# Key products of two edge groups: two 64-column products beside each other instead of two summed 128-column products with zeros

## The chip, the cores and the metric

The program runs on one core of one Trainium2 chip. Its engines work from queues of their own: TensorE (PE, with weight loads shown apart as PEld), VectorE (DVE), ScalarE (ACT), GpSimd (POOL), and SyncE (SP), which here only issues DMAs. They wait for one another through semaphores. The metric is the device time of one execution in microseconds. The kernel before takes 5307.28 us, the median of 3 runs (5303.45 to 5312.74).

## The reference, cut to what matters

A graph network with 6250 nodes and 206,250 edges (100,000 drawn edges, their mirror images and one loop for each node, sorted by destination). The first layer runs five rounds of message passing and a layer norm; the change doesn't touch it. The second layer is attention over edges:

```
def _conv_per_edge(x_src, edge_attr, edge_sh, Wang, Wlin, W1, b1, W2):
    rad = relu(edge_attr @ W1 + b1) @ W2          # b1: 64 wide, W2k: 64 x 64, W2v: 64 x 128
    g = edge_sh @ Wang.T
    return x_src * g @ Wlin * rad                 # Wlin_k: 128 x 64, Wlin_v: 128 x 128
k = _conv_per_edge(x[src], edge_attr, edge_sh, Wang_k, Wlin_k, W1k, b1k, W2k)   # keys, 64 per edge
v = _conv_per_edge(x[src], edge_attr, edge_sh, Wang_v, Wlin_v, W1v, b1v, W2v)   # values, 128 per edge
alpha = einsum('ehq,qk,ehk->eh', q[dst], Wdot, k)     # 8 heads
# softmax of alpha over the edges of one dst, then the weighted sum of v
```

So each edge has a key of 64 numbers, itself the elementwise product of two matrix products: the "radial" one, relu(...) @ W2k, and the "linear" one, (x * g) @ Wlin_k.

## The kernel before, in words

`edge_attention` works on 404 groups of 512 edges (GE = 512), with an edge in each column. Two groups make a pair, and there are 202 pairs. Since a key has 64 numbers and a tile has 128 partitions, the keys of a pair share a tile: those of the first group lie on partitions 0 to 63, those of the second on 64 to 127. From there on one instruction handles the keys of 1024 edges: the copy to `rad_k` (L2265), the products with `rad_k` and with the query (L2373, L2376), and the product that sums each head and puts it into a row of `b_s` (L2158).

To fill such a shared tile, TensorE does two products over all 128 columns of its array and sums them in the bank `b_k`. The weights stand in the middle of a tile of 192 columns with zeros on both sides. The slice for the first group has the 64 weight columns first and 64 zero columns after them, the slice for the second the other way round. `radial_k` (L2126) does this with `w2k` and `hidden` (rows 64 to 127 of `w2k` are zeros, because `hidden` holds the 64 hidden units of the keys and below them those of the values), `linear_k` (L2134) with `wlin_k` and `x_gk`. Both write `b_k`: the radial product of pair p is copied to `rad_k` by ACT, then the linear product of pair p takes the bank, and DVE reads it at L2373 (semaphore `p_lk` tells it that the product is done, `p_rk` tells the same of the radial product to ACT).

The order on every engine is written out by hand, pair by pair (`for i in range(LAST)`). For one pair TensorE does: turn the gathered rows (L2096), gates (L2105, L2108), hidden layer (L2114), linear keys of the pair before (L2134), turn an output (L2166), turn rows again, linear values (L2142), radial values (L2119), gates, turn queries (L2148), hidden layer, linear and radial values, head sums (L2158), turn an output, and radial keys (L2126). A 32-bit product of 512 columns shows as two MATMUL records, each with a LDWEIGHTS of its own; a call for both groups at L2126 or L2134 is thus four records.

Every 8 pairs a round of softmax work runs for 16 groups, mostly on DVE: scans (L2418, L2449, L2468, L2493), a reciprocal (L2499) and others. Four times in a round TensorE does a tiny product in between, at L2175 (`collect`) or L2183 (`hand_out`). Values wait 16 pairs for their weights and are then weighed and summed (L2394, L2402), so at the end there are 16 pairs' worth of such work without key products.

The built program marks each product with a piece of the array, as rows x columns. In the kernel before that is the whole array, 128 x 128, for every product of this stage but two: 128 x 32 at L2175 and 32 x 128 at L2183.

Of the kernel before, what the change touches and what calls it, by code (L numbers as in the profile page):

```python
# [18 lines left out]
P = 128  # L19
D = 128  # L20
DQ = 64
H = 8
EA = 16
HID = 64
# [1776 lines left out]
def edge_attention(nc, a, parts, x1_table, q_first, same_row, sums_table, ident, lent, G):  # L1801
# [31 lines left out]
    with ExitStack() as ctx:  # L1833
        def sb(name, shape, dt=F32):
            return ctx.enter_context(nc.sbuf_tensor(f"e_{name}", shape, dt))
# [11 lines left out]
        gates_part = [sb(f"gates_part{n}", [6 * EA, 3 * D], BF16) for n in range(3)]  # L1847
        gates_less = [sb(f"gates_less{n}", [6 * EA, 3 * D]) for n in range(2)]
        stack = sb("stack", [6 * EA, 3 * D], BF16)
        wlin_k = sb("wlin_k", [D, 3 * DQ])  # L1850
        wlin_v = sb("wlin_v", [D, D])
        b1 = sb("b1", [2 * HID, 1])
        w2k = sb("w2k", [2 * HID, 3 * DQ])
        w2v = sb("w2v", [2 * HID, D])
        ones = sb("ones", [P, P])
        gather_heads = sb("gather_heads", [P, 2 * P])
# [15 lines left out]
        hidden = several("hidden", 2, [2 * HID, GE])  # L1872
        x_gk = several("x_gk", 4, [D, GE])
# [33 lines left out]
        b_k = bank("b_k")  # L1907
# [65 lines left out]
        def _(sp):  # L1973
# [4 lines left out]
            for n, name in enumerate(("wang_k_t", "wang_v_t", "W1")):  # L1978
                for r in range(6):
                    sp.dma_start(gates[r * EA:(r + 1) * EA, n * D:(n + 1) * D], a[name]).then_inc(w_in, 16)  # L1980
            sp.wait_ge(const, 3)
            sp.dma_start(wlin_k[:, DQ:2 * DQ], a["Wlin_k"]).then_inc(w_in, 16)
            sp.dma_start(w2k[0:HID, DQ:2 * DQ], a["W2k"]).then_inc(w_in, 16)
            sp.dma_start(w2v[HID:2 * HID, :], a["W2v"]).then_inc(w_in, 16)
            sp.wait_ge(cut, 5)
            for n, r0, r1 in ((0, 0, 3), (1, 3, 4), (2, 4, 5), (1, 5, 6)):
# [62 lines left out]

        @block.gpsimd  # L2050
        def _(pool):
            nc.gpsimd.memset(wlin_k[:], 0.0).then_inc(const, 1)
            nc.gpsimd.memset(w2k[:], 0.0).then_inc(const, 1)
            nc.gpsimd.memset(w2v[:], 0.0).then_inc(const, 1)
            nc.gpsimd.memset(ones[:], 1.0).then_inc(const, 1)
            nc.gpsimd.memset(gather_heads[:], 0.0).then_inc(const, 1)
            nc.gpsimd.memset(minus_big[:], -BIG).then_inc(const, 1)
            nc.gpsimd.memset(across[0][:, 0:1], -BIG).then_inc(const, 1)
            nc.gpsimd.memset(wacross[0][:, 0:1], 0.0).then_inc(const, 1)
            pool.wait_ge(const, 8)  # L2060
            own_rows = gather_heads[:, P - ROWS:P]
            nc.gpsimd.affine_select(out=own_rows, in_=ones[:, 0:ROWS], compare_op=ALU.is_ge, fill=0.0, base=0,
                                    pattern=[[-H, ROWS]], channel_multiplier=1).then_inc(const, 1)
            pool.wait_ge(const, 9)
            nc.gpsimd.affine_select(out=own_rows, in_=own_rows, compare_op=ALU.is_ge, fill=0.0, base=H - 1,
                                    pattern=[[H, ROWS]], channel_multiplier=-1).then_inc(const, 1)
            nc.gpsimd.affine_select(out=row_of_head[:].rearrange("k (g h) -> k g h", h=H),
                                    in_=ones[0:H, :].rearrange("k (g h) -> k g h", h=H), compare_op=ALU.is_equal,
                                    fill=0.0, base=0, pattern=[[0, ROWS], [1, H]], channel_multiplier=-1
                                    ).then_inc(const, 1)  # L2070
            pool.wait_ge(w_in, n_w)
            for g in range(G):
                if g >= 3:
                    pool.wait_ge(p_x, g - 2)
                for j in range(GT):
                    nc.gpsimd.indirect_dma_start(  # L2076
                        x_rows[g % 3][:, j, :], None, x1_table,
                        bass.IndirectOffsetOnAxis(ap=src[:, g * GT + j:g * GT + j + 1], axis=0)
                        ).then_inc(x_got[g % 3], 16)

        @block.tensor
        def _(pe):
            pe.wait_ge(const, 11)
            nc.tensor.transpose(b_x[:, 0:H], row_of_head[:], ident[0:H, 0:H]).then_inc(p_small, 1)
            pe.wait_ge(w_in, n_w)
            pe.wait_ge(stacked, 64)
            pe.wait_ge(const, 12)

            def turn_x(g):
                pe.wait_ge(x_got[g % 3], 64 * (g // 3 + 1))  # L2090
# [30 lines left out]
            def radial_k(p):  # L2121
                pe.wait_ge(a_hid, 2 * p + 2)
                if p > 0:
                    pe.wait_ge(v_key, p)
                for half in range(2):
                    mm = nc.tensor.matmul(b_k[:], w2k[:, (1 - half) * DQ:(1 - half) * DQ + P], hidden[half][:],  # L2126
                                          start=(half == 0), stop=(half == 1))
                mm.then_inc(p_rk, 1)

            def linear_k(p):  # L2130
                pe.wait_ge(v_g, 4 * p + 3)
                pe.wait_ge(a_rk, p + 1)
                for half in range(2):
                    mm = nc.tensor.matmul(b_k[:], wlin_k[:, (1 - half) * DQ:(1 - half) * DQ + P],  # L2134
                                          x_gk[(2 * p + half) % 4][:], start=(half == 0), stop=(half == 1))
                mm.then_inc(p_lk, 1)

            def linear_v(g):
                pe.wait_ge(v_g, 2 * g + 2)
# [98 lines left out]
        @block.scalar  # L2238
        def _(act):
            act.wait_ge(w_in, n_w)  # L2240
            act.wait_ge(const, 8)

            def copy_x(g):
                act.wait_ge(p_x, g + 1)
# [4 lines left out]
            def hide(g):  # L2249
                act.wait_ge(p_hid, g + 1)  # L2250
                if g >= 2:
                    act.wait_ge(p_rk, g // 2)
                nc.scalar.activation(hidden[g % 2][:], b_r[:], ACT.Relu, bias=b1[:, 0:1]).then_inc(a_hid, 1)  # L2253

            def copy_rv(g):
# [3 lines left out]
                nc.scalar.copy(rad_v[g % 3][:], b_r[:]).then_inc(a_rv, 1)  # L2259

            def copy_rk(p):
                act.wait_ge(p_rk, p + 1)
                if p >= 2:
                    act.wait_ge(v_key, p - 1)
                nc.scalar.copy(rad_k[p % 2][:], b_k[:]).then_inc(a_rk, 1)  # L2265
# [64 lines left out]

        @block.vector
        def _(dve):
            dve.wait_ge(const, 8)
            dve.wait_ge(w_in, n_w)
            rest = gates
            for n in range(3):
# [13 lines left out]
            def gated(g):  # L2350
                dve.wait_ge(p_g, 2 * g + 1)
                dve.wait_ge(a_x, g + 1)
                if g >= 4:
                    dve.wait_ge(p_lk, g // 2 - 1)
                nc.vector.tensor_tensor(x_gk[g % 4][:], b_gk[:], x_t[g % 2][:], ALU.mult).then_inc(v_g, 1)  # L2355
                dve.wait_ge(p_g, 2 * g + 2)
                if g >= 4:
                    dve.wait_ge(p_lv, g - 3)
                nc.vector.tensor_tensor(x_gv[g % 4][:], b_gv[:], x_t[g % 2][:], ALU.mult).then_inc(v_g, 1)
# [6 lines left out]
                nc.vector.tensor_tensor(value[g % KEPT], b_lv[:], rad_v[g % 3][:], ALU.mult).then_inc(v_value, 1)  # L2366

            def products(p):
                dve.wait_ge(p_lk, p + 1)
                dve.wait_ge(a_rk, p + 1)  # L2370
                if p >= 2:
                    dve.wait_ge(p_score, p - 1)
                nc.vector.tensor_tensor(prod[p % 2][:], b_k[:], rad_k[p % 2][:], ALU.mult).then_inc(v_key, 1)  # L2373
                dve.wait_ge(v_key, p + 1)
                dve.wait_ge(v_query, 2 * p + 2)
                nc.vector.tensor_tensor(prod[p % 2][:], prod[p % 2][:], q_t[p % 2][:], ALU.mult).then_inc(v_prod, 1)  # L2376
# [259 lines left out]
```

## Time and profile before

| | |
|---|---|
| runs | 5303.45, 5307.28, 5312.74 us |
| the profiled execution's own time | 5309.66 us |
| its span in the trace | 5307.9 us |
| PE busy, share of the span | 4432.0 us, 83% |
| PE weight loads | 2894.7 us, 55% |
| DVE busy | 3888.6 us, 73% |
| ACT busy | 2422.2 us, 46% |
| POOL busy | 2022.3 us, 38% |
| edge attention, pair work | about 2510 to 5135 us of the span |

The shares are means over stages that have different limits. The change is inside the edge attention, so what matters is read there. A record of TensorE is longer than the time for which it holds the array: products are pipelined, so a product's cost in a full queue is the distance from its start to the next one's start, not its length. "Idle before" and the name behind the arrow tell how long an engine stood still and what ended that; small gaps of TensorE are hidden by the records' length.

### The profile page before, as it was taken

To read this page: it belongs to the slowest core of one execution; us is meant where nothing else is said; L and a number is where in the kernel's file an instruction comes from. 1 tells how busy PE (TensorE), PEld (TensorE's weight loads), DVE (VectorE), ACT (ScalarE), POOL (GpSimd) and SP (SyncE) were. 2 spreads that over 40 slices of the span, in tenths; PEclk is the share of its full clock that TensorE was granted. 3 is DMA by queue.
4 is the path that set the end of the run, shared out by engine and by line. 5 is a ranking of instruction groups with operands and counts; after the bars stand their busy time and mean duration, and the time that the engine had idled before them with its cause. 6 is when DMAs were issued, how large, how long until landed. Compare 5 with 4: busy or idle time off the path is not lost. (4 is left out here: it accounts for less than half of the span.)

```text
span 5307.9 us, 66619 instructions
## 1 busy us (share of the span) xinstructions
PE 4432.0 (83%) x19382; PEld 2894.7 (55%) x19382; DVE 3888.6 (73%) x6001; ACT 2422.2 (46%) x3740; POOL 2022.3 (38%) x1942
## 2 busy tenths in 40 slices
PE   4666689899999999741999999999999999999823
PEld 4666577777777777630445445544544454544412
DVE  7999654545545454441689999999998999999945
ACT  5666555554545545330444444444444444444411
POOL 3333000000000000015766666666666666766422
PEclk9888899999999999855999999999999999999955
DMA  3333699998999989403599999999999999999961
GB/s 109 103 103 101 143 221 219 197 229 184 222 193 222 227 182 232 83 0 79 140 230 249 256 246 257 249 247 254 254 246 241 251 248 244 256 247 241 241 179 35
DMA packets 1847237, 1043.13 MB, mean 197 GB/s; under 512 B 1316550, under 2 KB 1666372, under 8 KB 1846892
## 3 DMA queue, kind: packets, MB, share of 16 engines
q1 hardware_dynamic: 1441835, 700.05, 59.8%
q10 hardware_dynamic: 344208, 211.90, 13.7%
q0 software_dynamic: 60848, 127.02, 9.1%
q8 instruction: 163, 2.67, 0.2%
q14 instruction: 183, 1.49, 0.1%
HBM read 763.53 MB, written 274.94 MB: 196 GB/s over the span
## 5 line engine op out<-in xcount | busy, mean ns | idle before, releaser
L2076 POOL DMA_INDIRECT e_x_rows<-x_table,e_src x1616 | 1682.5, 1041 | 824.5 <-issue 438.9
L1144 PE MATMUL acc<-t_wide,scaled 128*128 128x512 f32 (+1 forms) x6370 | 1466.2, 388 | 120.5 <-DVE t_wide L1281 75.6
L1144 PEld LDWEIGHTS acc<-t_wide,scaled 128*128 128x128 f32 x6370 | 1165.7, 191 | 406.9 <-ACT t_wide L1162 137.6
L1162 ACT CAST t_wide<-t_ring 128x1176 fp32r<-128x1176 uint8 (+1 forms) x490 | 597.0, 1255 | 303.1 <-PE acc L1144 212.9
L1281 DVE CAST t_wide<-t_ring 128x1764 fp32r<-128x1764 uint8 (+1 forms) x490 | 535.0, 1124 | 223.5 <-PE acc L1144 220.2
L1647 POOL MEMSET l_eps<- 128x1 f32 x2 | 0.2, 102 | 1648.3 <-POOLq L1347 1639.6
L2402 DVE TENSOR_TENSOR_SCAN e_vsum<-e_factors,e_vsum,e_weighted 128x512 f32<-128x512 f32 x403 | 519.2, 1288 | 14.2
L539 PE MATMUL lists_rows_ps<-lists_hot_lo,lists_hot_hi 128*128 128x196 fp8e4 x3200 | 377.4, 286 | 177.3 <-DVE lists_hot_hi L464 177.3
L2271 ACT COPY e_out_rows<-e_b_o 128x512 f32<-128x512 f32 x404 | 236.8, 586 | 564.4 <-PE e_b_o L2166 436.9
L2142 PE MATMUL e_b_lv<-e_x_gv,e_wlin_v 128*128 128x512 f32 x808 | 431.1, 615 | 72.6 <-DVE x_res L2366 38.2
L1291 DVE TENSOR_TENSOR e_less<-e_x,e_part 128x512 f32<-128x512 f32 x101 | 69.9, 692 | 548.9 <-ACT e_part L1184 336.6
L539 PEld LDWEIGHTS lists_rows_ps<-lists_hot_lo,lists_hot_hi 128*128 128x128 fp8e4 x3200 | 338.4, 110 | 215.7 <-DVE lists_hot_hi L464 198.7
L2119 PE MATMUL e_b_r<-e_hidden,e_w2v 128*128 128x512 f32 x808 | 445.6, 634 | 0.8 <-ACT e_hidden L2253 0.8
L2259 ACT COPY e_rad_v<-e_b_r 128x512 f32<-128x512 f32 x404 | 237.0, 587 | 425.2 <-PE e_b_r L2119 425.0
L2355 DVE TENSOR_TENSOR e_x_gk<-e_b_gk,e_x_t 128x512 f32<-128x512 f32 x404 | 275.3, 681 | 170.0 <-PE e_b_gv L2108 115.6
L2134 PE MATMUL e_b_k<-e_x_gk,e_wlin_k 128*128 128x512 f32 x808 | 385.4, 599 | 13.2 <-ACT e_rad_k L2265 13.0
L330 ACT CAST lists_staged<-lists_rows_ps 128x784 uint8<-128x784 f32 x400 | 312.5, 812 | 183.8 <-PE lists_rows_ps L539 183.0
L2126 PE MATMUL e_b_k<-e_hidden,e_w2k 128*128 128x512 f32 x808 | 380.3, 593 | 0.0
L2166 PEld LDWEIGHTS e_b_o<-ident,e_vsum 128*128 128x128 f32 x1616 | 208.0, 148 | 313.7 <-issue 176.9
L2253 ACT ACTIVATE e_hidden<-e_b_r,e_b 128x512 f32<-128x512 f32 x404 | 278.9, 690 | 146.7 <-PE e_b_r L2114 144.4
L2247 ACT COPY e_x_t<-e_b_x 128x512 f32<-128x512 f32 x404 | 237.8, 589 | 223.2 <-PE e_b_x L2096 131.4
L2166 PE MATMUL e_b_o<-ident,e_vsum 128*128 128x128 f32 x1616 | 262.9, 288 | 88.0 <-DVE e_vsum L2402 37.9
(207 smaller groups left out, 6250.4 us busy)
## 6 DMA issues: line engine op xcount, KB each, us to landing
e_factors<-share_rows SPq DMA_DIRECT2D x404, 512.0 KB
sums_table<-e_out_rows ACTq DMA_DIRECT2D x404, 256.0 KB
t_ring<-adjacency_bytes SPq DMA_DIRECT2D x245, 416.5 KB, 6.2
t_ring<-adjacency_bytes SPq DMA_DIRECT2D x245, 367.5 KB, 4.8
q_first<-hop_zeros_q ACTq DMA_DIRECT2D x101, 512.0 KB, 4.5
e_q_rows<-q_first SPq DMA_DIRECT2D x404, 128.0 KB
e_same_dst<-same_row SPq DMA_DIRECT2D x404, 128.0 KB
adjacency_bytes<-lists_staged SPq DMA_DIRECT2D x196, 196.0 KB, 2.7
```

What stands on the lines that cost most here:

```text
L330: nc.scalar.copy(staged[g % 3][:, at * half:(at + 1) * half, :], rows_ps[t % 3][:, :, 0:2 * LO]).then_inc(evicted, 1)
L539: mm = nc.tensor.matmul(rows_ps[t % 3][:, side, col * LO:(col + 1) * LO], his[:, i * P - i % 2 * SLOTS:i * P - i % 2 * SLOTS + P], los[:, ...
L1144: mm = nc.tensor.matmul(acc[c][:, 0:n], U[p][:, b, :], flat_t[:, lo:lo + n], start=(b == 0 and p == 0), stop=(b == NB - 1 and p == 1), ski ...
L1162: nc.scalar.copy(wide[g % WIDE][:, h0:h1, :], ring[g % BYTES][:, h0:h1, :]).then_inc(wide_act, 1)
L1281: nc.vector.tensor_copy(wide[g % WIDE][:, 0:h1, :], ring[g % BYTES][:, 0:h1, :]).then_inc(wide_dve, 1)
L2076: nc.gpsimd.indirect_dma_start(x_rows[g % 3][:, j, :], None, x1_table, bass.IndirectOffsetOnAxis(ap=src[:, g * GT + j:g * GT + j + 1], axis=0)
L2119: nc.tensor.matmul(b_r[:], w2v[:], hidden[g % 2][:], start=True, stop=True).then_inc(p_rv, 1)
L2126: mm = nc.tensor.matmul(b_k[:], w2k[:, (1 - half) * DQ:(1 - half) * DQ + P], hidden[half][:], start=(half == 0), stop=(half == 1))
L2134: mm = nc.tensor.matmul(b_k[:], wlin_k[:, (1 - half) * DQ:(1 - half) * DQ + P], x_gk[(2 * p + half) % 4][:], start=(half == 0), stop=(half ...
L2142: nc.tensor.matmul(b_lv[:], wlin_v[:], x_gv[g % 4][:], start=True, stop=True).then_inc(p_lv, 1)
L2166: tr = nc.tensor.transpose(b_o[:, j * P:(j + 1) * P], vsum[g % 3][:, j * P:(j + 1) * P], ident[:])
L2402: nc.vector.tensor_tensor_scan(out=vsum[g % 3][:], data0=factors[g % FACTORS][:, 1, :], data1=weighted[g % 2][:], initial=vsum[(g - 1) % 3 ...
```

## The change

The tiles `wlin_k` and `w2k` lose their zeros: `wlin_k` is now 128 x 64, `w2k` 64 x 64. Each half of the pair is a product of its own with 64 output partitions: the first group's goes to partitions 0 to 63 of `b_k`, the second group's to 64 to 127. Nothing is summed in the bank any more, and each half raises the semaphore, so that the waits on `p_rk` and `p_lk` count twice as far. The built program marks the radial halves with pieces of 64 x 64 at row 0, columns 0 and 64, and the linear halves with pieces of 128 x 64 at columns 0 and 64. The number of columns that stream (512 for each half) is as before, and so is the number of products.

No instruction changes place on PE, DVE, ACT or SP; on POOL two memsets fall away at the start of the stage, with the counts on `const`.

```diff
-        wlin_k = sb("wlin_k", [D, 3 * DQ])
+        wlin_k = sb("wlin_k", [D, DQ])
-        w2k = sb("w2k", [2 * HID, 3 * DQ])
+        w2k = sb("w2k", [HID, DQ])
...
-            sp.wait_ge(const, 3)
-            sp.dma_start(wlin_k[:, DQ:2 * DQ], a["Wlin_k"]).then_inc(w_in, 16)
-            sp.dma_start(w2k[0:HID, DQ:2 * DQ], a["W2k"]).then_inc(w_in, 16)
+            sp.wait_ge(const, 1)
+            sp.dma_start(wlin_k[:], a["Wlin_k"]).then_inc(w_in, 16)
+            sp.dma_start(w2k[:], a["W2k"]).then_inc(w_in, 16)
...
-            nc.gpsimd.memset(wlin_k[:], 0.0).then_inc(const, 1)
-            nc.gpsimd.memset(w2k[:], 0.0).then_inc(const, 1)
             nc.gpsimd.memset(w2v[:], 0.0).then_inc(const, 1)
...
                 for half in range(2):
-                    mm = nc.tensor.matmul(b_k[:], w2k[:, (1 - half) * DQ:(1 - half) * DQ + P], hidden[half][:],
-                                          start=(half == 0), stop=(half == 1))
-                mm.then_inc(p_rk, 1)
+                    nc.tensor.matmul(b_k[half * DQ:(half + 1) * DQ, :], w2k[:], hidden[half][0:HID, :], start=True,
+                                     stop=True).then_inc(p_rk, 1)
...
                 for half in range(2):
-                    mm = nc.tensor.matmul(b_k[:], wlin_k[:, (1 - half) * DQ:(1 - half) * DQ + P],
-                                          x_gk[(2 * p + half) % 4][:], start=(half == 0), stop=(half == 1))
-                mm.then_inc(p_lk, 1)
+                    nc.tensor.matmul(b_k[half * DQ:(half + 1) * DQ, :], wlin_k[:], x_gk[(2 * p + half) % 4][:],
+                                     start=True, stop=True).then_inc(p_lk, 1)
...
-                    act.wait_ge(p_rk, g // 2)
+                    act.wait_ge(p_rk, 2 * (g // 2))
...
-                act.wait_ge(p_rk, p + 1)
+                act.wait_ge(p_rk, 2 * p + 2)
...
-                    dve.wait_ge(p_lk, g // 2 - 1)
+                    dve.wait_ge(p_lk, 2 * (g // 2 - 1))
...
-                dve.wait_ge(p_lk, p + 1)
+                dve.wait_ge(p_lk, 2 * p + 2)
```

## Rows read from the trace of the kernel before

**Rows 1.** Busy time by stretch of the span, columns in the first line.
```profile
core 0: us, PE busy (x) PEld busy (x) DVE busy (x) ACT busy (x) POOL busy (x), PEclk, DMA share, GB/s
2620.00:5020.00 2400.00, 2287.09 (x8595) 1183.94 (x8594) 2212.13 (x3220) 1073.65 (x1837) 1594.59 (x1526) 0.98 1.00 246
```
**Rows 2.** TensorE in order of time: start, us, line, out<-in, shape, count.
```profile
4001.58 1.13 PE L2119 MATMUL e_b_r<-e_hidden,e_w2v 128*128 128x512 f32 x2
4002.54 1.02 PE L2158 MATMUL e_b_s<-e_prod,e_gather_heads 128*128 128x512 f32 x2
4003.40 0.60 PE L2166 MATMUL e_b_o<-ident,e_vsum 128*128 128x128 f32 x4
4003.84 1.88 PE L2126 MATMUL e_b_k<-e_hidden,e_w2k 128*128 128x512 f32 x4
4005.56 0.60 PE L2096 MATMUL e_b_x<-ident,e_x_rows 128*128 128x128 f32 x4
...
4006.64 1.88 PE L2134 MATMUL e_b_k<-e_x_gk,e_wlin_k 128*128 128x512 f32 x4
4008.36 0.60 PE L2166 MATMUL e_b_o<-ident,e_vsum 128*128 128x128 f32 x4
```
**Rows 3.** Timeline of the weight loads beside the first of these.
```profile
4003.73 0.30 PEld L2126 LDWEIGHTS e_b_k<-e_hidden,e_w2k 128*128 128x128 f32 x2
4004.27 0.19 PEld L2126 LDWEIGHTS e_b_k<-e_hidden,e_w2k 128*128 128x128 f32 x1 [0.24 <-issue]
```
**Rows 4.** Timeline of TensorE around the gates, without a tiny product.
```profile
3999.77 0.38 PE L2108 MATMUL e_b_gv<-e_sh_t,e_stack 96*128 96x512 bf16 x1
3999.98 0.60 PE L2148 MATMUL e_b_x<-ident,e_q_rows 128*128 128x128 f32 x4
```
**Rows 5.** Timeline of TensorE one pair later, with one (L2175).
```profile
4010.10 1.02 PE L2119 MATMUL e_b_r<-e_hidden,e_w2v 128*128 128x512 f32 x2
4010.95 0.38 PE L2105 MATMUL e_b_gk<-e_sh_t,e_stack 96*128 96x512 bf16 x1
4011.18 0.38 PE L2108 MATMUL e_b_gv<-e_sh_t,e_stack 96*128 96x512 bf16 x1
4011.48 0.21 PE L2175 MATMUL e_b_o<-e_ends,e_head_of_row 128*8 128x16 f32 x2
4011.62 0.66 PE L2148 MATMUL e_b_x<-ident,e_q_rows 128*128 128x128 f32 x4
```
**Rows 6.** Timeline of VectorE over one round: all its waits of 0.1 us or more.
```profile
4090.37 0.69 DVE L2355 TENSOR_TENSOR e_x_gk<-e_b_gk,e_x_t 128x512 f32<-128x512 f32 x1 [2.19 <-PE e_b_gv L2108]
...
4101.65 0.69 DVE L2355 TENSOR_TENSOR e_x_gk<-e_b_gk,e_x_t 128x512 f32<-128x512 f32 x1 [1.12 <-PE e_b_gv L2108]
...
4124.58 0.69 DVE L2355 TENSOR_TENSOR e_x_gk<-e_b_gk,e_x_t 128x512 f32<-128x512 f32 x1 [0.64 <-PE e_b_gv L2108]
...
4127.96 0.69 DVE L2366 TENSOR_TENSOR feats<-e_b_lv,e_rad_v 128x512 f32<-128x512 f32 x1 [0.17 <-PE e_b_lv L2142]
...
4161.36 0.69 DVE L2355 TENSOR_TENSOR e_x_gk<-e_b_gk,e_x_t 128x512 f32<-128x512 f32 x1 [0.90 <-PE e_b_gv L2108]
...
4164.74 0.69 DVE L2366 TENSOR_TENSOR feats<-e_b_lv,e_rad_v 128x512 f32<-128x512 f32 x1 [0.17 <-PE e_b_lv L2142]
```
**Rows 7.** The same for TensorE, the gaps that its records leave open.
```profile
4142.37 1.10 PE L2142 MATMUL e_b_lv<-e_x_gv,e_wlin_v 128*128 128x512 f32 x2 [0.63 <-DVE feats L2366]
...
4157.79 0.66 PE L2166 MATMUL e_b_o<-ident,e_vsum 128*128 128x128 f32 x4 [0.91 <-DVE e_wacross L2478]
...
4181.33 1.92 PE L2142 MATMUL e_b_lv<-e_x_gv,e_wlin_v 128*128 128x512 f32 x2 [2.61 <-DVE x_res L2366]
```
**Rows 8.** Busy time of three stretches of that round, columns as in Rows 1.
```profile
4084.00:4128.00 44.00, 43.91 (x168) 23.18 (x167) 39.25 (x59) 20.82 (x36) 28.86 (x27) 0.98 1.10 265
...
4164.70:4181.30 16.60, 14.00 (x56) 7.05 (x54) 16.35 (x22) 7.06 (x12) 12.58 (x13) 1.00 0.82 228
4181.30:4187.70 6.40, 6.37 (x14) 2.94 (x15) 6.22 (x9) 1.17 (x2) 1.18 (x2) 0.73 0.83 196
```
**Rows 9.** Waits in the stretch 2620 to 5020: in total, times, longest.
```profile
SPq L1993 <- PE e_b_r L2114: 946.5, 165, 12.6
...
POOL e_x_rows L2076 <- PE e_b_x L2096: 372.3, 175, 7.2
...
ACT e_out_rows L2271 <- DMA sums_table<-e_out_rows: 84.2, 39, 5.0
```
**Rows 10.** Timeline of the start of the stage.
```profile
2490.56 0.26 POOL L2052 MEMSET e_wlin_k<- 128x192 f32 x1 [11.27 <-POOLq L1522]
2490.76 0.26 POOL L2053 MEMSET e_w2k<- 128x192 f32 x1
...
2500.82 0.42 SPq L1982 DMA_DIRECT2D e_wlin_k<-in_Wlin_k  x1
```

More of the change, by code:

```diff
@@ L2059, in _ @@
             nc.gpsimd.memset(wacross[0][:, 0:1], 0.0).then_inc(const, 1)
-            pool.wait_ge(const, 8)
+            pool.wait_ge(const, 6)
             own_rows = gather_heads[:, P - ROWS:P]
@@ L2063, in _ @@
                                     pattern=[[-H, ROWS]], channel_multiplier=1).then_inc(const, 1)
-            pool.wait_ge(const, 9)
+            pool.wait_ge(const, 7)
             nc.gpsimd.affine_select(out=own_rows, in_=own_rows, compare_op=ALU.is_ge, fill=0.0, base=H - 1,
@@ L2082, in _ @@
         def _(pe):
-            pe.wait_ge(const, 11)
+            pe.wait_ge(const, 9)
             nc.tensor.transpose(b_x[:, 0:H], row_of_head[:], ident[0:H, 0:H]).then_inc(p_small, 1)
@@ L2086, in _ @@
             pe.wait_ge(stacked, 64)
-            pe.wait_ge(const, 12)
+            pe.wait_ge(const, 10)
             def turn_x(g):
@@ L2240, in _ @@
             act.wait_ge(w_in, n_w)
-            act.wait_ge(const, 8)
+            act.wait_ge(const, 6)
             def copy_x(g):
@@ L2332, in _ @@
         def _(dve):
-            dve.wait_ge(const, 8)
+            dve.wait_ge(const, 6)
             dve.wait_ge(w_in, n_w)
```

## The prediction

> **What bounds the kernel now.** The change lives in the pair work of the edge attention, so I first read the busy time by stretch [rows 1]. From 2620 to 5020 us TensorE is busy 2287 of 2400 us, VectorE 2212, and the DMA share is 1.00. All three are nearly full, so neither engine's share alone says what a shorter product is worth. Next come the waits of the two engines over one round of 8 pairs, 4084 to 4187 us [rows 6, 7]. An engine that waits shows that the other one is the limit just before. VectorE waits for TensorE at 4090, 4101, 4124 and 4161 (2.19, 1.12, 0.64, 0.90 us). TensorE waits for VectorE at 4142, 4157 and 4181 (0.63, 0.91, 2.61 us). The limit therefore changes hands inside a round: TensorE sets the pace from 4084 to 4128, where it is busy 43.91 of 44.00 us [rows 8], and from 4157.8 to 4164.7; VectorE sets it in the other stretches, with its scans and its reciprocal. The waits of the other queues come last [rows 9]: SP waits 946 us for TensorE before it loads more features, POOL 372 us, so transfers mostly follow TensorE. Only the output stores hold somebody up (84 us in 39 waits).
>
> **What a pair of key products costs now.** In a full queue the distance between starts counts, not the length. L2126 starts at 4003.84, the next line at 4005.56: 1.72 us for four records, 0.43 each; L2134 has the same, 4006.64 to 4008.36 [rows 2]. The next record's weight load lies under the running one (loads at 4003.73 and 4004.27, [rows 3]) and costs nothing. There are two such sets in a pair, so 3.44 us of some 12 us.
>
> **What the change does to the streams.** It leaves the number of records and their 512 columns. A half that uses 64 of 128 columns of the array streams as long as before. Time is saved only if the array runs records of the two halves at the same time. A half is two records on the same piece of the array, which must follow each other (0.43 + 0.43). Records start in the order of the queue: first half, first half, second half, second half. So the third can start beside the second at best, the fourth after the third: three steps of 0.43 = 1.29 instead of 1.72. Saved: 0.43 a set. If the third record's 64-column weight load can't be taken in earlier, it comes on top. A 128-column load that isn't hidden costs 1.13 - 1.02 = 0.11 us (L2119 after a wait against L2119 in a full queue, [rows 2, 5]); half the columns make it 0.05. The trace has no two pieces at work at once; the bounds are 1.29 (all overlaps as said) and 1.72 (nothing does).
>
> **What the change adds: switching the piece.** The trace has this already, at the tiny products. Without one, L2148 follows L2108 after 0.21 us [rows 4]. With L2175 in between it follows after 0.44 us, and the four L2148 take 0.66 instead of 0.60, a load that isn't hidden: together the detour costs 0.29 us [rows 4, 5]. Of this the streaming is two records of 16 columns, 2 x 0.43 x 16/512 = 0.03. The rest, 0.26, is two changes of piece, with an 8-column load open on the way in. A 64-column load is some 0.04 dearer by the 0.11 above. So 0.30 us for going in and out, at each set. The neighbours of a set are always whole-array products: L2166 or L2158 before L2126, L2096 after it, L2114 before L2134, L2166 or L2096 after it. Between the halves nothing else stands, and I take no change there. The bounds of this term are 0.26 and, if each entry and exit cost the whole detour, 0.58; the nearest row gives 0.30, and that I take. Before, none of it was paid.
>
> The page TensorEngine Tiling (Array Packing) of the Trainium skill, section Tiling Modes, says that changing the mode, not just the piece, drains the engine. By that rule the same four drains a pair come out, and the trace agrees with its 0.29. The same page's table of theoretical speedup promises up to 2x for a side of 64; that would halve the 1.72 and is a rival below.
>
> **The sum.** A set goes from 1.72 to 1.29 + 0.30 = 1.59, or 1.64 with the third load open: saved 0.08 to 0.13, say 0.10 us. In the round above, the sets (L2126 and L2134, eight each) that lie where TensorE sets the pace are eight between 4084 and 4128 and two between 4157.8 and 4164.7: 10 of 16. The other six end in a TensorE wait for VectorE, which only gets longer. There are 202/8 = 25.25 rounds: 10 x 0.10 x 25.25 = 25 us, bounds 20 and 33. VectorE can follow: what is taken is its own waits, 5.2 us a round. If all 16 sets counted, at 0.13, it would be 53 us.
>
> Other edits: two memsets of 0.26 us leave POOL at 2490.56, where SP comes to L1982 only at 2500.82, long after [rows 10]: nothing. The doubled semaphore counts move no wait, since every waiting instruction still waits for the second half. The order of the queues is as before. The copy of `rad_k` and the DVE products start 0.1 us sooner: inside the sum.
>
> The profiled execution took 5309.66 us, of which 5307.9 are the span; the median is 2.4 below it. 5309.7 - 25 = 5284.7, and by the median 5282.
>
> **The rivals.**
> Rival 1, slower: the array doesn't run the halves at the same time. The place is again the queue of TensorE at L2126 and L2134: four steps of 0.43, plus 0.30, so 2.02 instead of 1.72 a set. Where TensorE sets the pace that is 10 x 0.30 x 25.25 = 76 us: 5383. For the other six sets the waits of 0.63, 0.91 and 2.61 [rows 7] cover two sets each (0.60). If they don't, 121 us: 5428. In the other direction, the long wait is followed by half the clock: granted 0.73 over 6.40 us, so 3.5 us at 1.2 GHz and some 1.7 us lost [rows 8]; before it TensorE stood for 2.61 us. If a wait of 2.0 no longer drops the clock, 43 us come back: 5340. The side changes where overlap saves less than 0.30 of the 0.43. For this rival: no row shows two products at once. Against: loads and products already overlap freely [rows 3].
> The page TensorE: Matmul & The Clock Gate, Part 3, says that a weight load overlaps running products only when it goes to other rows of the array. The two halves use the same rows, so by this rule the second half's load would wait for the first half's stream, and nothing is left to overlap: this rival's time. The trace speaks against the rule as far as it goes, since L2126's load at 4004.27 runs under a product on the same rows [rows 3].
>
> Rival 2, no change: the overlap is there, but no weight load is hidden on a piece of the array. One of the four is in the 0.30; the other three add 3 x 0.05: 1.29 + 0.30 + 0.15 = 1.74. Or the gain is there and transfers take it: in the stretch where TensorE sets the pace the DMA share is 1.10 at 265 GB/s against 0.82 at 228 where VectorE does [rows 8], and the stores' waits grow. Against the second: SP's 946 us of waiting for TensorE [rows 9]. Time: 5300 to 5314.
>
> Rival 3, much faster: the two halves fully beside each other, 0.86 + 0.30 = 1.16, saved 0.56 a set: 141 us, 5166. That is what the page's factor of 2 gives. Against it: the records of one half follow each other in the queue.
>
> **How the numbers follow.** Forecast (three steps) 0.47, its own range 5250 to 5297; rival 1 0.35; rival 2 0.14; rival 3 0.04. A measurement of this kernel can tell 0.2%, 10.6 us. Faster by more: 0.45 of the forecast and rival 3, 0.49. Within: rival 2 and the forecast's edge, 0.16. Slower: 0.35. The range takes in the forecast from all sets counted (5254) and rival 1 up to a little short of its upper bound: 5254 to 5412.
>
> **What would show it.** In a timeline of TensorE after the change: starts of the four records of L2126. Forecast: the third starts within 0.05 us of the second, and from the first record to the next line it is about 1.5 us, with open gaps of about 0.1 before and after the set. Rival 1: starts 0.43 apart, and about 2.0. Rival 3: all within 0.9. Next the waits: VectorE's waits at L2355 [rows 6] shrink under the forecast (5.2 us in the round, by about 1) and grow by 3 under rival 1; TensorE's waits for VectorE go the other way. The granted clock after the long wait tells whether rival 1 gets time back. I would be wrong in the step "the third starts beside the second" if starts stay 0.43 apart, in the step "0.30 for in and out" if gaps of another size stand there, and in the count of 10 of 16 if a set's saving and the total don't go together.

## The result, and the profile after

The changed kernel takes 5276.6 us (median of 11 runs, 5255.2 to 5292.3), the kernel before on the same chip 5303.5 us (11 runs): ratio 0.9947, 95% interval [0.9933, 0.9962], so 27 us or 0.5% faster. The forecast was 5282. The profiled execution took 5255.19 us with a span of 5253.5; it is the fastest of its runs, 21 us under their median, while the profiled execution before was 6 us above its own. So the two profiles lie 54 us apart, twice the difference of the medians, and what is read from the pair of them is somewhat too large.

First the busy time of the two stretches that answer to [rows 1] and to the end of [rows 8] (columns as there).
```profile
2620.00:5020.00 2400.00, 2121.78 (x8633) 977.41 (x8632) 2245.39 (x3267) 1078.04 (x1849) 1608.75 (x1523) 0.96 1.02 250
4050.70:4057.00 6.30, 6.30 (x19) 2.90 (x20) 6.15 (x9) 1.58 (x3) 1.11 (x2) 0.75 0.85 201
```
TensorE is busy 165 us less than in [rows 1] while it does slightly more of the work (VectorE 3267 instructions against 3220); its mean clock fell from 0.98 to 0.96. The long wait and the low clock after it are still there, as in [rows 8].

The timeline of TensorE around the two sets, columns as in [rows 2].
```profile
4002.91 0.63 PE L2162 MATMUL e_b_o<-ident,e_vsum 128*128 128x128 f32 x4
4003.47 1.08 PE L2124 MATMUL e_b_k<-e_hidden,e_w2k 64*64 64x512 f32 x4
4004.47 0.65 PE L2094 MATMUL e_b_x<-ident,e_x_rows 128*128 128x128 f32 x4
...
4006.62 1.08 PE L2131 MATMUL e_b_k<-e_x_gk,e_wlin_k 128*64 128x512 f32 x4 [0.84 <-ACT e_rad_k L2261]
4007.63 0.66 PE L2162 MATMUL e_b_o<-ident,e_vsum 128*128 128x128 f32 x4
```
From the start of the set at L2124 to the next line it is 1.00 us where [rows 2] have 1.72. Going in costs the product before it 0.56 - 0.44 = 0.12 us (4002.91 to 4003.47, against 4003.40 to 4003.84), going out another 0.65 - 0.60 = 0.05. Together 1.17 against 1.72: 0.55 us saved a set. (Over all 202 radial sets the last record before a set is 0.09 us longer by the medians, 203 against 109 ns to the set's start; the 0.12 of this place holds 0.03 that is not the entry.)

The set at L2131 starts 3.15 us after the one at L2124, where [rows 2] have 2.80, although the first set is 0.55 us shorter. Its 0.84 us of waiting for `rad_k` goes back to ScalarE, whose queue stands before the copy of an output:
```profile
4004.81 0.59 ACT L2267 COPY e_out_rows<-e_b_o 128x512 f32<-128x512 f32 x1 [1.97 <-DMA sums_table<-e_out_rows]
```

How the four records lie, from the same timeline cut to four narrow windows. The view shows what runs in a window, so the count at the end of the line grows as records start.
```profile
4003.47 0.64 PE L2124 MATMUL e_b_k<-e_hidden,e_w2k 64*64 64x512 f32 x1
...
4003.47 0.65 PE L2124 MATMUL e_b_k<-e_hidden,e_w2k 64*64 64x512 f32 x2
...
4003.47 1.07 PE L2124 MATMUL e_b_k<-e_hidden,e_w2k 64*64 64x512 f32 x3
```
The windows are 4003.46 to .47, 4003.471 to .93 and 4003.94 to .95. Two records are there within 0.01 us of each other, nothing is added for 0.46 us, then the other two come (x4 with the same 1.08 in the window from 4003.95). Over 191 such sets the median starts are 0, 7, 480 and 487 ns. Each half raises the semaphore with its last record, and it is the records at 480 and 487 that raise it: so the first two are the first records of the two halves, and the halves run fully side by side. The weight loads of this set, four within one burst, the last two (by the medians 55 and 62 ns after the first) under the products that already run:
```profile
4003.47 0.19 PEld L2124 LDWEIGHTS e_b_k<-e_hidden,e_w2k 64*64 64x64 f32 x4 [0.17 <-issue]
```

The gaps that TensorE leaves open in one round (4050 to 4145), against [rows 7].
```profile
4050.66 2.05 PE L2138 MATMUL e_b_lv<-e_x_gv,e_wlin_v 128*128 128x512 f32 x2 [2.61 <-DVE e_value L2362]
...
4082.78 1.97 PE L2131 MATMUL e_b_k<-e_x_gk,e_wlin_k 128*64 128x512 f32 x4 [4.49 <-ACT e_rad_k L2261]
...
4113.51 1.10 PE L2138 MATMUL e_b_lv<-e_x_gv,e_wlin_v 128*128 128x512 f32 x2 [1.95 <-DVE feats L2362]
...
4125.00 1.10 PE L2138 MATMUL e_b_lv<-e_x_gv,e_wlin_v 128*128 128x512 f32 x2 [0.86 <-DVE feats L2362]
...
4128.93 0.66 PE L2162 MATMUL e_b_o<-ident,e_vsum 128*128 128x128 f32 x4 [1.12 <-DVE e_wacross L2474]
```
The waits for VectorE are of the sizes of [rows 7]; the 4.49 us for ScalarE's `rad_k` has no match in that round (over 2620 to 5020 such waits sum to 13.0 us before, the longest 3.0). Its origin, in the timeline of all engines:
```profile
4080.97 0.59 ACT L2267 COPY e_out_rows<-e_b_o 128x512 f32<-128x512 f32 x1 [5.59 <-DMA sums_table<-e_out_rows]
...
4082.05 0.59 ACT L2261 COPY e_rad_k<-e_b_k 128x512 f32<-128x512 f32 x1 [0.49 <-ACT e_out_rows L2267]
...
4083.21 0.69 DVE L2351 TENSOR_TENSOR e_x_gk<-e_b_gk,e_x_t 128x512 f32<-128x512 f32 x1 [3.10 <-ACT e_x_t L2243]
...
4086.44 1.78 PE L2138 MATMUL e_b_lv<-e_x_gv,e_wlin_v 128*128 128x512 f32 x2
```
ScalarE stands 5.59 us before it copies a result into one of two output buffers, because the store of that buffer hasn't landed. `rad_k`, next in its queue, is late, TensorE stands, VectorE too, and afterwards L2138 takes 1.78 us for two records that took 1.02: the granted clock is 0.50 from 4082.8 to 4088. The waits in the stretch 2620 to 5020, against [rows 9] (total, times, longest):
```profile
POOL e_x_rows L2074 <- PE e_b_x L2094: 281.5, 112, 6.7
ACT e_out_rows L2267 <- DMA sums_table<-e_out_rows: 200.8, 84, 6.5
...
DVE e_x_gk L2351 <- PE e_b_gv L2106: 55.4, 43, 2.9
PE e_b_lv L2138 <- DVE x_res L2362: 49.7, 26, 2.6
PE e_b_k L2131 <- ACT e_rad_k L2261: 41.4, 32, 5.4
```
The stores' waits went from 84 to 201 us. Of all the gaps of TensorE over 0.15 us in this stretch, those that VectorE ends grew from 91 to 177 us and those that ScalarE ends from 20 to 82 (sums over the trace). The period of a pair by its place in the round (start of the radial set to the next one, medians over pairs 26 to 197, worked out from the trace) shows what arrives:
```
place    0      1      2      3      4      5      6      7
before  11.41  12.00  11.87  12.09  12.81  11.87  15.96  11.41
after   10.29  12.51  10.78  12.29  12.82  10.78  16.17  10.28
```
Four places are 1.1 us shorter, which is two sets of 0.55 each; the other four are as long or longer. In the round of [rows 6] the pairs that begin at 4086, 4098, 4109, 4121 and 4158 are the places 7, 0, 1, 2 and 5, and they hold the prediction's ten sets: place 1 is among them and did not get shorter. The mean round, 98.3 us against 100.3, is less shortened than the medians, since stalls like the one above fall into single pairs. TensorE stood at 1.2 GHz during the pair work, from the first radial set to the last, for 95.6 us before and 170.7 after.

### The profile page after: what moved, and what is told of

The parts are those of the page before. It is cut to its first block and busy times, and to the rows that moved or that the text cites. A ratio compares the mean times of both kernels' runs of the same rounds, so it can differ in the third digit from the quotient of the medians.

```text
span 5253.5 us, 66617 instructions
## 1 busy us (share of the span) xinstructions
PE 4238.7 (81%) x19382; PEld 2663.2 (51%) x19382; DVE 3884.3 (74%) x6001; ACT 2420.7 (46%) x3740; POOL 2038.0 (39%) x1940
## 5 line engine op out<-in xcount | busy, mean ns | idle before, releaser
L2138 PE MATMUL e_b_lv<-e_x_gv,e_wlin_v 128*128 128x512 f32 x808 | 443.8, 632 | 106.5 <-DVE x_res L2362 49.7
L2162 PEld LDWEIGHTS e_b_o<-ident,e_vsum 128*128 128x128 f32 x1616 | 192.8, 150 | 385.6 <-issue 229.0
L2162 PE MATMUL e_b_o<-ident,e_vsum 128*128 128x128 f32 x1616 | 277.1, 297 | 96.8 <-DVE e_vsum L2398 36.0
L1184 ACT CAST e_part<-e_less 128x512 bf16<-128x512 f32 x202 | 125.1, 619 | 372.1 <-issue 313.6
L2094 PEld LDWEIGHTS e_b_x<-ident,e_x_rows 128*128 128x128 f32 x1616 | 180.3, 142 | 214.9 <-issue 182.3
```

The costliest lines, as they stand in the source:

```text
L2138: nc.tensor.matmul(b_lv[:], wlin_v[:], x_gv[g % 4][:], start=True, stop=True).then_inc(p_lv, 1)
L2162: tr = nc.tensor.transpose(b_o[:, j * P:(j + 1) * P], vsum[g % 3][:, j * P:(j + 1) * P], ident[:])
```

## The experiments

They ran in three groups, each on a chip of its own, with the kernel before beside every group. Beside one group (the changed kernel again, with four buffers, and VectorE relieved) it took 5300.4 us, close to the 5303.5 above; I call that and the comparison above the first chip. Beside the other two groups it took 5646.4 and 5635.4; these are the second and the third chip, the slower ones. So ratios are compared, and absolute differences only within a chip. The changed kernel by itself, with two buffers and nothing else altered, ran on the first chip only.

**One set alone.** The radial set in halves as in the change, the linear set over the whole array as before.
The edit against the kernel before:
```
                 for half in range(2):
-                    mm = nc.tensor.matmul(b_k[:], w2k[:, (1 - half) * DQ:(1 - half) * DQ + P], hidden[half][:],
...
+                    nc.tensor.matmul(b_k[half * DQ:(half + 1) * DQ, :], w2k[:], hidden[half][0:HID, :], start=True,
+                                     stop=True).then_inc(p_rk, 1)
```


> Only the radial set (L2126) is done in pieces of the array; the linear set stays as two whole-array products with zeros. Theory (the two halves run fully beside each other, 1.16 us a set with going in and out, and what is left of the gain is lost to VectorE's stretches and to ACT's waits for the output stores): the radial set takes 1.0 us from first start to the next line, the linear set still 1.72, a pair that TensorE paces falls from 11.4 to about 10.85 us, and the total is 10 to 25 us under the kernel before. Rival (the granted clock takes the gain, since TensorE now waits longer and falls to half speed more often): the same set times, but the mean clock of the pair work falls below 0.98 and the total is within 5 us of before.

Measured on the second chip 5607.9 against 5646.4, ratio 0.9933 [0.9903, 0.9963], 38 us, more than the 10 to 25 expected. TensorE's timeline, first the one set, then the other:
```profile
4128.35 1.08 PE L2125 MATMUL e_b_k<-e_hidden,e_w2k 64*64 64x512 f32 x4
4129.35 0.66 PE L2095 MATMUL e_b_x<-ident,e_x_rows 128*128 128x128 f32 x4
...
4133.01 1.95 PE L2132 MATMUL e_b_k<-e_x_gk,e_wlin_k 128*128 128x512 f32 x4 [2.35 <-issue]
4134.80 0.60 PE L2164 MATMUL e_b_o<-ident,e_vsum 128*128 128x128 f32 x4
```
1.00 us to the next line in halves, 1.79 whole in this set, which begins after a wait; over all 202 sets the medians are 1.01 and 1.72. The saving belongs to each set by itself. The clock did what the rival said, a mean of 0.93 in the stretch 2620 to 5020, but the total did not stay within 5 us of before.

ScalarE hardly waits for a store in this run, though it has two buffers (2620 to 5020):
```profile
ACT e_out_rows L2269 <- DMA sums_table<-e_out_rows: 4.0, 2, 2.3
```
In the two runs of the next experiment, also with two buffers and on the slower chips, it is 0 and 3.1 us. So on these chips there is next to no wait for stores that four buffers could take away.

**Both halves on the same piece.** The edit keeps the smaller products and the switching and takes only the overlap away; both halves go to columns 0 to 63, so the keys of the second group are left out.
```
-                    nc.tensor.matmul(b_k[half * DQ:(half + 1) * DQ, :], w2k[:], ...)
+                    nc.tensor.matmul(b_k[0:DQ, :], w2k[:], ...)
-                    nc.tensor.matmul(b_k[half * DQ:(half + 1) * DQ, :], wlin_k[:], ...)
+                    nc.tensor.matmul(b_k[0:DQ, :], wlin_k[:], ...)
```


> The changed kernel with both halves of a set sent to the same piece of the array (partitions 0 to 63 of the bank; the keys of the second group are left out, and the bank is written once at the start). Same number of products, columns and changes of piece, but no two pieces to run at once. Theory: the four records start 0.43 us apart, a set takes 2.0 us with going in and out, and the total is 60 to 120 us above the kernel before (10 to 16 sets of a round, 0.30 us each). Rival (a 64-column product is simply shorter by itself, whatever piece it goes to): starts under 0.3 us apart, total as the changed kernel, 25 us under before.

> Both halves of a set on the same piece of the array (the keys of the second group are left out), measured again because the first comparison ran on a chip where the kernel before took 5646 us. Theory: 5.3 ms again for before, four starts 0.43 apart, a set of 2.0 us, and 60 to 120 us over the kernel before. Rival (a longer set hides behind VectorE's and the stores' waits, as the 1.0006 of the slow chip says): within 20 us of before.

Measured 1.0006 [0.9974, 1.0038] on the second chip and 1.0021 [0.9997, 1.0046] on the third. The set, in TensorE's timeline:
```profile
4134.82 0.60 PE L2164 MATMUL e_b_o<-ident,e_vsum 128*128 128x128 f32 x4
4135.35 1.93 PE L2126 MATMUL e_b_k<-e_hidden,e_w2k 64*64 64x512 f32 x4
4137.20 0.66 PE L2094 MATMUL e_b_x<-ident,e_x_rows 128*128 128x128 f32 x4
```
1.85 us to the next line, 0.53 - 0.44 = 0.09 on the way in and 0.06 on the way out: 2.00, rival 1's 2.02. So it is the other columns that let the halves run together, and the switching costs 0.28 us: 0.15 at the neighbours (0.09 + 0.06) and 1.85 - 1.72 = 0.13 inside the set. Of this 0.05 is a step of 0.48 between its first two records, where the following steps are 0.43. The total did not follow: 0.28 us a set, dearer than before, cost next to nothing on these chips, where I had expected 60 us or more. Yet on the same second chip a shorter radial set alone brought 38 us. These runs don't show why the one counts and the other doesn't; the last section has an argument for it. What rival 1 would have cost on the first chip wasn't run.

**Four output buffers in place of two.** This takes away what ScalarE waits for. Room for them came from laying start-up buffers over later ones and merging two semaphores into another, in both kernels.
```
-        out_rows = several("out_rows", 2, [P, GT, D])
+        out_rows = several("out_rows", 4, [P, GT, D])
-                if g >= 2:
-                    act.wait_ge(stored[g % 2], 16 * (g // 2))
+                if g >= 4:
+                    act.wait_ge(stored[g % 4], 16 * (g // 4))
```


> The changed kernel with four output buffers in place of two, so that ACT waits for the store of four groups ago and not of two (room is made by letting start-up tiles share memory, two semaphores are merged into another). Theory (stores hold ACT and through it TensorE, 201 us of ACT waits against 84 in the kernel before): ACT's waits for the stores fall under 40 us in the stretch 2620 to 5020, and the total is 40 to 100 us under the changed kernel's 5276.6, so 1.3 to 2.4% under before. Rival (transfers as a whole are the limit, or the clock takes it): the waits turn up at other loads or at the clock, and the total is within 10 us of the changed kernel.

> The kernel before with the same four output buffers. Theory: it waits less for stores (84 us in ACT), so it gains less from the buffers than the changed kernel: 10 to 35 us under the kernel before, and the difference between changed and before grows from 27 us to 60 to 100 us once both have four buffers. Rival (transfers or clock are the limit): both gain the same, and the difference stays at 20 to 35 us.

> The kernel before with four output buffers, beside the others. Theory (two output buffers cost the changed kernel more, since it comes to its stores sooner): 15 to 40 us under before, so that with four buffers the change is worth 60 to 90 us, against the 27 to 34 with two. Rival (the buffers help both alike): 60 us or more under before.

On the second chip the changed kernel with four buffers took 0.9839 [0.9792, 0.9886] and the kernel before with four 0.9959 [0.9929, 0.9989], 22 us less, as expected; on the third chip the kernel before with four took 0.9963 [0.9939, 0.9986], 12 us where 15 to 40 were expected. With four buffers in both, the change is worth 1.2% on the second chip, 5624.7 - 5556.2 = 68 us. This does not show that the buffers set the saving free there: stores held nobody up with two either, and the changed kernel with two buffers was not run beside them.

The same on the first chip, with the changed kernel beside it once more:

> The changed kernel itself, beside the others on one chip (in the last comparison the kernel before took 5646 us, against 5303 in the first). Theory (a set of products is 0.56 us shorter wherever the kernel runs; what is left of it depends on what else holds the engines): sets as in the first trace (1.0 us from the first start to the next line), total 0.3 to 1.2% under before. Rival (the gain of 0.5% holds only on the first chip): within 0.2% of before.

> The changed kernel with four output buffers, now beside the changed kernel. Theory (stores hold ACT): 0.6 to 1.6% under the changed kernel, with ACT's waits for the stores cut to less than half. Rival (the buffers only helped against that chip's disturbances, or nothing): within 0.3% of the changed kernel.

The changed kernel 5266.9, 0.9931 [0.9914, 0.9947]; with four buffers 5199.2, 0.9803 [0.9790, 0.9815]. The 68 us between them are twice what the change alone brought (33.5), as the theory for both runs had it. Here, on the first chip, there were waits for stores to take away. In the stretch 2620 to 4900, with four buffers:
```profile
2620.00:4900.00 2280.00, 2077.25 (x8502) 950.50 (x8501) 2180.61 (x3186) 1067.54 (x1818) 1611.23 (x1524) 0.97 1.05 257
```
ScalarE has no wait for a store left in it, where the changed kernel in the run beside it has
```profile
ACT e_out_rows L2267 <- DMA sums_table<-e_out_rows: 191.4, 78, 6.3
```
and the transfers got quicker, not slower, 257 GB/s against 251. The median periods at the eight places are 10.28, 12.50, 10.78, 13.14, 12.06, 10.78, 16.17 and 10.28: the same four are short, and places 3 and 4 together are no shorter than before (25.20 against 24.90). What went is the stalls in single pairs: the mean round is 96.2 us, the sum of these medians 96.0. This is the fastest version found that computes everything, 2.0% under the kernel before. How much of it four buffers bring without the change was measured on the slower chips only (0.4%, where no store held ScalarE). On the first chip the kernel before had 84 us of such waits, so part of the 2.0% may be had there without the change; that run is missing.

**VectorE relieved.** If VectorE's stretches eat the saving, a VectorE with less to do must let it through. In both kernels two of its steps were cut, which leaves results out: the reciprocal of each round to a copy, and the product with the queries of each pair to one column.
```
-                nc.vector.tensor_tensor(prod[p % 2][:], prod[p % 2][:], q_t[p % 2][:], ALU.mult).then_inc(v_prod, 1)
+                nc.vector.tensor_tensor(prod[p % 2][:, 0:1], prod[p % 2][:, 0:1], q_t[p % 2][:, 0:1], ALU.mult).then_inc(v_prod, 1)
-                nc.vector.reciprocal(local[0:n, :], local[0:n, :]).then_inc(v_round, 1)
+                nc.vector.tensor_copy(local[0:n, :], local[0:n, :]).then_inc(v_round, 1)
```


> The kernel before with less work on VectorE: the reciprocal of each round is a copy, and the product of the keys with the query takes one column in place of 512 (both leave results out). That is some 2.7 + 8 x 0.5 = 6.7 us less a round of 99. TensorE's work is as before, 8 x 11.25 = 90 us a round plus the waits. Theory (VectorE sets the pace in part of each round, TensorE in the rest): 3 to 8 us a round are saved, 75 to 200 us in all, and pairs settle near 11.4 us, paced by TensorE.

> The changed kernel with the same relief for VectorE. Theory (in the changed kernel VectorE's stretches eat most of the gain): with VectorE relieved the changed kernel is 60 to 170 us faster than the kernel before with the same relief, more than twice the 27 us between the two without it. Rival (stores and transfers eat it): the difference between the two stays at 15 to 40 us, and ACT's waits for the stores grow instead.

Measured on the first chip 5197.8 (0.9810 [0.9793, 0.9828]) without and 5194.3 (0.9790 [0.9777, 0.9803]) with the change: 3.5 us apart, which the intervals hardly tell from nothing. The theory wanted 60 to 170 us and the rival 15 to 40. The busy time of 2620 to 4900 and then the waits for the stores, without the change:
```profile
2620.00:4900.00 2280.00, 2226.88 (x8543) 1165.73 (x8542) 2046.01 (x3202) 1064.55 (x1828) 1539.61 (x1520) 1.00 1.04 258
```
The waits in the same stretch:
```profile
ACT e_out_rows L2271 <- DMA sums_table<-e_out_rows: 172.7, 68, 6.2
```
The busy time with the change:
```profile
2620.00:4900.00 2280.00, 2065.49 (x8551) 963.38 (x8550) 2038.59 (x3202) 1062.28 (x1827) 1649.12 (x1526) 0.98 1.05 258
```
And its waits:
```profile
ACT e_out_rows L2267 <- DMA sums_table<-e_out_rows: 319.1, 112, 7.0
```
TensorE is busy 161 us less for the same work, and ScalarE waits 146 us more for stores. The theory that VectorE alone swallows the gain falls. The rival was wrong in its size and right in its sign, the growing waits for stores. Without the change VectorE was worth 103 us, though, so it does hold the kernel before.

**Both taken away.** Relief and four buffers, without and with the change, on the third chip.

> The kernel before with VectorE relieved (reciprocal as a copy, query product of one column; both leave results out) and four output buffers. Theory A (with two buffers the stores were what held the relieved kernels at 5195 us): no wait for stores, pairs at 11.4 to 11.9 us paced by TensorE, 5140 to 5170 us. Theory B (transfers as a whole hold them, 258 GB/s): within 15 us of 5198.

> The changed kernel with VectorE relieved and four output buffers: the place where the whole saving should show, if TensorE paces it. Theory A: 80 to 170 us under the kernel before with the same two edits (the full saving is 16 x 0.56 = 9 us a round, 226 in all, less where VectorE with 87 us a round takes over), so 5000 to 5080 us. Theory B (transfers): within 20 us of 5194, at 258 to 262 GB/s, with waits at other loads in place of the stores.

Measured 5605.9 (0.9957 [0.9923, 0.9991]) and 5483.4 (0.9720 [0.9685, 0.9754]): 122 us or 2.2% apart, within the 80 to 170 us expected of the pair. On the first chip the change alone brought 33.5 us, and 3.5 with only VectorE relieved. The busy time of 2620 to 4900, first without the change:
```profile
2620.00:4900.00 2280.00, 1994.92 (x7274) 1023.39 (x7272) 1745.21 (x2721) 903.07 (x1554) 1358.80 (x1307) 0.96 0.87 219
```
and with it:
```profile
2620.00:4900.00 2280.00, 1941.48 (x7588) 890.49 (x7587) 1813.55 (x2838) 943.33 (x1622) 1450.39 (x1364) 0.93 0.92 228
```
So in one setting the change brings several times the 27 us. The number to hold it against is not the 139 us (0.55 x 10 x 25.25) of the ten sets: with VectorE relieved the other six count too, which gives 0.55 x 16 x 25.25 = 222 us, and 122 is somewhat over half of that. Nor does the pair show which of the two edits lets the saving through. It ran on the third chip, where no store held ScalarE with two buffers either (3.1 us), and neither edit was made there alone with the change. Without the change the two edits bring 0.4% there, where VectorE's relief alone brought 1.9% on the first chip; both theories for that run had expected some 2 to 3%. The absolute times were expected as on the first chip and are not comparable. Whether that pair would open as far on the first chip stays open: the three quickest kernels there all end within 5 us of each other at 257 to 258 GB/s, which may be what the transfers allow.

## Why the prediction was right in its number and wrong in two steps

**"The third can start beside the second at best" failed.** The step assumed that records start in the order of the queue, first half, first half, second, second. The trace has the first record of either half at once and the second record of either half 0.48 us later. Instead of three steps of 0.43 there are two, and the run with both halves on one piece shows that it is the other columns that do it. Rival 3 had this mechanism and its set of 1.16 us; 1.17 were measured. I gave it 0.04, which was too little: no row spoke on the order of records on two pieces, and the only argument was the queue. The table of the Trainium skill, TensorEngine Tiling (Array Packing), section Theoretical Speedup, gives up to 2x for a side of 64; for the streaming that holds here, 0.86 for 1.72, without the switching. The rule in the Trainium skill, TensorE: Matmul & The Clock Gate, Part 3, that a weight load overlaps running products only when it goes to other rows, doesn't hold here: all the products of a set use the same rows, and two of its four loads start 55 and 62 ns after the first, under products that run on for another 0.4 us.

**"0.30 in and out" held.** In is 0.12 (0.09 by the medians), out 0.05, and the first records of the halves have an open load, 0.64 where a streamed record takes 0.59. With the gap that the next line waits, the set is 1.17 = 0.86 + 0.31. That is the 0.30 taken from the tiny products. The run on one piece has 2.00 = 1.72 + 0.28.

**"10 of 16 sets" failed, in the other direction.** 0.55 x 10 x 25.25 = 139 us should have come out; 27 and 33.5 us did, a fifth to a quarter on the first chip. The count treated a stretch where TensorE sets the pace as one that keeps doing so after 4 us have been taken from it. Where it went, by what the runs show and, where said, by argument:
- Stores. Rival 2 named it ("transfers take it ... the stores' waits grow") and held it for a small thing because SP waited 946 us for TensorE. But the transfer that counted was not SP's: it is the store that ScalarE waits for with two buffers, and ScalarE's queue also holds `rad_k`. Taking that wait away in the changed kernel gave 68 us on the first chip.
- The clock. 75 us more at 1.2 GHz; at half the speed that is at most some 37 us lost, an estimate from these two numbers that takes TensorE to set the pace all that time. With four buffers it is 136.5 us, in the changed kernel beside it 191.1, so about half of the 75 to 95 us hangs on the stalls. No run changed the clock alone.
- VectorE. Half of the eight places did not get shorter, with four buffers either (3 and 4 taken together). With four buffers TensorE's gaps that VectorE ends sum to 233 us in 2620 to 5020 (91 before, 177 in the changed kernel), those that ScalarE ends to 15. Of the 139 us, 33.5 + 68 = 101 are found with four buffers, if the kernel before gained nothing from them, which wasn't run on this chip; the other 38 or more are what is left for VectorE and the clock. How these two share them wasn't separated.

So two wrong terms cancelled: the saving of a set was 0.10 where it is 0.55, and ten sets were counted where some two carry it to the end. 5282 against 5276.6 is luck in size; right by reasoning are only the sign and the price of switching. That the other edits cost nothing was not tested by itself.

**VectorE's waits at L2355** should have shrunk by about 1 us of 5.2 a round. They fell from 95.3 to 55.4 us over the stretch, 1.7 a round, for the larger saving. Rival 1, 0.35 by itself, had the right set time for a kernel without overlap (2.00 in the run with one piece), and the wrong price: there its 0.28 a set cost 0.1 to 0.2% on the slower chips, within the noise, not 1.4. On the first chip it wasn't run.

## What to carry to other kernels

When a queue's operation gets shorter by x, count it for the total only as long as the next limit stays away: look how far each waiting engine is ahead, and above all at waits that are already there on a third engine, however small their sum. A wait of 84 us for stores with two buffers became 201 us as soon as TensorE got faster; in the changed kernel two more buffers were worth twice the change itself. Two 32-bit products of 512 columns that need 64 columns of the array each, two records each, took 1.17 us side by side for 1.72, in and out included.

## What the runs showed of the hardware that I had not expected

Products on different columns run record by record together, 7 ns apart, although the program gives the whole of the first before the second. Four records on one piece stay one after the other (starts at 0, 0.48, 0.91 and 1.34 us, 1.85 to the next line).

On the two slower chips signals of TensorE often arrive late. In the kernel with one set in halves, all engines, 4021 to 4028:
```profile
4021.62 0.38 PE L2113 MATMUL e_b_r<-e_ea_t,e_stack 96*128 96x512 bf16 x1
...
4026.23 0.16 DVE L2382 COPY e_q_t<-e_b_x 128x1 f32<-128x1 f32 x1 [2.15 <-remote]
4026.27 0.69 ACT L2251 ACTIVATE e_hidden<-e_b_r,e_b 128x512 f32<-128x512 f32 x1 [5.02 <-remote]
4026.31 0.50 SPq L1995 DMA_DIRECT2D e_sh_t<-parts_sh  x1
...
4027.01 2.08 PE L2118 MATMUL e_b_r<-e_hidden,e_w2v 128*128 128x512 f32 x2 [4.15 <-ACT e_hidden L2251]
```
The product ends at 4022.00; ScalarE, which needs nothing else, starts at 4026.27, and VectorE and SP go on in the same 0.1 us. Counted from the traces, 2620 to 4900: in the profiles of this chip and the third one 1498 to 1988 of some 3000 to 3500 records of TensorE that raise a semaphore saw its next rise over 0.5 us after their end, on the first chip 36 to 71 of some 3400 to 3900. Stretches of over 1.3 us in which nothing starts sum to 30 to 73 us there and to at most 2.2 us on the first. That a set longer by 0.28 us costs next to nothing there would follow if TensorE waits for such signals anyway; this is argued, not shown, and the 38 us that one shorter set brought on the second chip don't fit it well. Transfers aren't the cause of the stretch shown, their share being 0.23 in it; what is stays open.
